# Score maxima two by two in TensorE's order, and none between the halves of the product with V

## Chip, cores and metric

The kernel runs on one core of one Trainium2 chip, as one launch. The metric is device time in microseconds (us). A core has five engines with instruction streams of their own, which meet only at semaphores: TensorE (PE in the profile), VectorE (DVE), ScalarE (ACT), GpSimd (POOL) and SyncE (SP), which issues most DMAs.

## The reference, cut to what matters

The input is 8 rows of 512 tokens by 128 features. Each row goes through two attentions with 16 heads of 8 dimensions, both of them computed from the same normalized tokens, and one of them is followed by a mixture of one shared and eight routed experts.

```python
for each of the 8 rows x:                      # x: 512 x 128
    xn = layernorm(x)
    # attention 1: causal, weights 1 - tanh(energy)**2, divided by their sum, then @ Wo.T
    s  = attention_1(xn)
    # attention 2: full softmax over 512 keys, then + residual
    h  = rmsnorm(xn, norm1_w)
    X  = xn + softmax(q @ k.T * scale) @ v @ wo
    # feed-forward: shared expert + 8 experts, top 2 weighted by the router
    h2 = rmsnorm(X, norm2_w)
    g  = X + shared(h2) + sum_e combine[:, e] * (silu(h2 @ gate_e) * (h2 @ up_e)) @ down_e
    out = x + s * silu(g)
```

The softmax of attention 2 subtracts the maximum of each query's scores before the exponential. These maxima are what the change moves.

## The kernel before

**A row's stages on TensorE.** The kernel loops over the 8 rows. The first seven run in a hardware loop (`LOOP`, it = 0 to 6), the last one stands behind it (`LAST`), and a short prologue (`FIRST`) prepares row 0. Within a row TensorE's program has 28 attention units and then 9 experts.

Units 0 to 15 are attention 2 (stage 1): unit n computes, for 4 heads and one block of 128 keys, the transposed scores in two halves q of two heads each (`scores`, L951, two 64-row matmuls into S0 or S1, the heads r = 0 and r = 1 of a head pair at partitions 0 to 63 and 64 to 127), ScalarE takes the exponential (L522), and the product with V (`with_v`, L976) follows two units later. For most units that product is itself cut in two halves of 256 columns, each behind one half of the scores. Units 16 to 27 are attention 1 (stage 2), with the causal mask added by matmuls (L943) and VectorE forming the weights (L684); there the product with V is one piece, behind the first half of the scores.

An expert (`expert`) is 12 matmuls of 512 columns with all 128 rows, in four groups of three (L1013, L1014, L1015: the high and low parts of a split multiplication), and each group is one step. From expert 2 on, the second product of the expert two before it (L997) follows as steps 5 and 6, so that an expert has 6 steps, and 4 for experts 0 and 1.

**The maxima.** The maximum over 512 keys must be known before stage 1 of a row. `maximum` on TensorE (L918) multiplies Q and K of one head h and one tile t of 128 queries, 48 rows by 512 columns, into M0 or M1, and VectorE reduces the 512 columns to one (L647). A row has 64 of them (16 heads by 4 tiles), in the order of head pair, tile, head r: run X (head pairs 0 to 3, 32 maxima) is computed for the next row during the experts, and the runs Y and Z (head pairs 4 and 5, and 6 and 7, 16 maxima each) for this row in units 0 to 8. Neighbours in the order have different r: they read partitions 0 to 47 and 64 to 111. The finished maxima of a run are turned by one matmul (`maxT_X`, `maxT_Y`, `maxT_Z`, L924) and go by DMA into a row of Q's stack, so that the score matmul itself subtracts them.

**The two M buffers.** All small products of TensorE go through M0 and M1 in turn: the maxima, the projections, transposes of the outputs (`oT2`, `oT1`, L930), the router's logits (L1084), a suffix sum of V (`suffix`, L1090), the routing weights' transpose (`combT`, L1097). `begin` waits until the use two before has been read, and stops TensorE's whole stream there, since an engine works its program in order:

```python
k, _n = u(name)                  # M0 or M1, by turns
pe.wait_ge(*free(u, name))       # the use before the last has been read
```

**Placement.** The table `PLACES` gives the list of small works of each unit and expert; its order fixes the turns of M0 and M1 and the order in which VectorE and ScalarE read. Where inside a unit or expert a work stands in TensorE's order is decided in `row`, by cutting the list into as many pieces as there are steps, four in a unit. The lists of an X expert are: expert 2: x0 to x4; expert 3: oT1 2, oT1 3, x5 to x8; expert 4: x9, x10, V1, x11, ctxT1, x12; expert 5: x13, x14, proj1, x15 to x17; experts 6 and 7: six maxima each; expert 8: x30, x31, maxT_X. (x0 is the first maximum of run X.) VectorE reads the first 4 of a list of 6 ahead of its own product of an expert (L792), and the last 2 behind it.

Of the kernel before, what the change touches and what calls it, by code (L numbers as in the profile page):

```python
# [132 lines left out]
def program(nc, x, par, n1w, n2w, w1, w2, router, w_gu, w_dn, out):  # L133
# [4 lines left out]
    with ctx_:  # L138
# [745 lines left out]
        def _(pe):  # L884
# [48 lines left out]
            def scores(it, n, q):  # L933

                k, c = score_use(it, 2 * n + q)
                pe.wait_ge(s_read[k], c + 1)
                g, _kind, js = ATTENTION[n]
                key, query = ("K2", "Q2") if n < N1 else ("K1", "Q1")
                hp, at = 2 * g + q, 0
                if n >= N1:  # L940
                    for j in js:
                        for r in range(2):
                            t_.matmul(S[k][:, 512 * r + at:512 * r + at + 128], identb[:, :], never[:, :],  # L943
                                      start=(j == js[0]), stop=False, skip_group_check=True)
                        at += L - 128 * j
                    at = 0
                for j in js:
                    i0 = 0 if n < N1 else 128 * j
                    for r in range(2):
                        rows = slice(HALF * r, HALF * r + HALF)  # L950
                        last = t_.matmul(S[k][:, 512 * r + at:512 * r + at + L - i0],  # L951
                                         stack[key][rows, hp, 128 * j:128 * j + 128],
                                         stack[query][rows, hp, i0:L], start=n < N1, stop=True, skip_group_check=n >= N1)
                    at += L - i0
                last.then_inc(s_full[k], 1)

            def with_v(it, n, half=None):


                g, _kind, js = ATTENTION[n]  # L960
                G, V, w = (g, V2, width(n)) if n < N1 else (NG + g, V1, width(n))
                k, c = acc_use(it, G)
                if js[0] == 0:
                    pe.wait_ge(o_read[k], c + 1)
                if n >= N1:
                    pe.wait_ge(weighed, it * WEIGHED + 2 * (n - N1) + 2)
                elif half != 1:
                    for i in range(2):
                        pe.wait_ge(s_read[i], it * S_USES + n + 2)
                at = 0  # L970
                for j in js:
                    i0, i1 = (128 * j if n >= N1 else 0, L) if half is None else (half * L // 2, (half + 1) * L // 2)
                    if n < N1:
                        at = i0
                    for q in range(4):
                        last = t_.matmul(O[k][32 * q:32 * q + VW, i0:i1], V[:, j, 4 * g + q, :],  # L976
                                         PT[:, n % SLOTS, w * q + at:w * q + at + i1 - i0],
                                         start=(j == 0), stop=(NT - 1 in js and j == js[-1] and half != 0))
                    at += i1 - i0
                if half != 0:  # L980
                    last.then_inc(pv_done, 1)

            def routing_weights(it, e):
                k, c = acc_use(it, 2 * NG + 2 * e - 1)
                pe.wait_ge(o_read[k], c + 1)
                t_.matmul(O[k][:, :], sel[:, e - 1, :], cT[:, :], start=True, stop=True).then_inc(cb_full, 1)  # L986
# [119 lines left out]
            def first_scores(it):  # L1106

                pe.wait_ge(row_in["X"], (it + 1) * 64)
                for q in range(2):
                    scores(it, 0, q)  # L1110

            def row(u, it, following):
                order.clear()
                current[0] = u

                v_at = {n: n - 2 for n in range(2, N1 + 2)} | {n: n - 3 for n in range(N1 + 3, UNITS)}
                for n in range(UNITS):
                    if n == N1 - 1:
                        pe.wait_ge(setup, 2)
                    for run, (p0, _p1) in RUNS.items():  # L1120
                        if n == NT * (p0 // 2) and n:
                            pe.wait_ge(row_in[run], (it + 1) * 64)
                    if n == N1:
                        for name in ("Q1", "K1"):
                            pe.wait_ge(stacked[name], (it + 1) * 32 * len(PAIRS))
                    names = u.places[n]
                    for i in range(4):
                        if i % 2 == 0:
                            if n:
                                scores(it, n, i // 2)  # L1130
                        elif v_at.get(n, N1) < N1 and v_at[n] % NT > 0:
                            with_v(it, v_at[n], i // 2)
                        elif n in v_at and i == 1:
                            with_v(it, v_at[n])
                        for name in names[len(names) * i // 4:len(names) * (i + 1) // 4]:
                            work(u, it, name)
                with_v(it, UNITS - 3)
                pe.wait_ge(h2r_ready, it + 1)
                for e in range(NE):
                    names = u.places[EXPERT + e]  # L1140
                    steps = 6 if e >= 2 else 4
                    for i, _step in enumerate(expert(it, e)):
                        if e == 0 and i < 2:
                            with_v(it, UNITS - 2 + i)
                        for name in names[len(names) * i // steps:len(names) * (i + 1) // steps]:
                            work(u, it, name)
                routing_weights(it, NE - 1)
                for _step in second_product(it, NE - 2):
                    pass
                for t in range(NT):  # L1150
                    last = t_.matmul(O[0][:, t * 128:t * 128 + 128], x1[:, t, :], ident[:, :], start=False, stop=False)
                last.then_inc(down_done, 1)
                for _step in second_product(it, NE - 1):
                    pass
                if following:
                    first_scores(it + 1)
                work(u, it, "outT")
                assert order == u.order
# [8 lines left out]
            with pe.Fori(0, B - 1) as it:  # L1167
                row(LOOP.row(it), it, True)
            row(LAST, B - 1, False)


# [37 lines left out]
```

## Time and profile before

| | |
|---|---|
| median of 3 runs | 1283.97 us (1280.16 to 1283.98) |
| profiled execution, its own time | 1285.18 us |
| its span, first to last instruction | 1283.4 us |
| PE busy | 1141.4 us, 89% |
| DVE busy | 870.5 us, 68% |
| ACT busy | 687.7 us, 54% |
| POOL busy | 342.0 us, 27% |
| granted TensorE clock over the span | 0.939 of full speed |

A row of the batch takes 153.6 us on TensorE. "L918 MATMUL M<-stackK,stackQ" is the instruction at line 918 that writes M from the stacks of K and Q. A row of the timeline with "x4" holds four like instructions, and its duration is from the first one's start to the last one's end. "[0.79 <-DVE nmax L647]" says that the engine sat idle for 0.79 us until that instruction of VectorE released it. Matmul records begin when the matmul begins to stream, and last longer than the time after which the next one begins, because the array is a pipeline; the distance between starts is what counts.

### The profile page before, as it was taken

To read this page: it belongs to the slowest core of one execution; us is meant where nothing else is said; L and a number is where in the kernel's file an instruction comes from. 1 tells how busy PE (TensorE), PEld (TensorE's weight loads), DVE (VectorE), ACT (ScalarE), POOL (GpSimd) and SP (SyncE) were. 2 spreads that over 40 slices of the span, in tenths; PEclk is the share of its full clock that TensorE was granted. 3 is DMA by queue.
4 is the path that set the end of the run, shared out by engine and by line. 5 is a ranking of instruction groups with operands and counts; after the bars stand their busy time and mean duration, and the time that the engine had idled before them with its cause. 6 is when DMAs were issued, how large, how long until landed. Compare 5 with 4: busy or idle time off the path is not lost.

```text
span 1283.4 us, 21377 instructions
## 1 busy us (share of the span) xinstructions
PE 1141.4 (89%) x7176; PEld 493.3 (38%) x7176; DVE 870.5 (68%) x1702; ACT 687.7 (54%) x937; POOL 342.0 (27%) x180
## 2 busy tenths in 40 slices
PE   2379999899998899899998999989999899999998
PEld 1112454234541354324543245422454234542365
DVE  7366975669757686576865688656976568756682
ACT  4039822597226862378523883249722596227842
POOL 6400542014320333203421035210542014420013
PEclk9559999799997999989998999979999799998999
DMA  5510330004300042002310034000440004300000
GB/s 165 99 36 2 76 70 5 27 2 87 62 1 27 24 82 44 11 18 43 70 37 27 2 62 75 13 28 2 75 74 1 27 9 84 58 1 18 1 1 8
DMA packets 58626, 49.95 MB, mean 39 GB/s; under 512 B 6672, under 2 KB 58128, under 8 KB 58384
## 3 DMA queue, kind: packets, MB, share of 16 engines
q1 hardware_dynamic: 55744, 44.35, 18.1%
q10 hardware_dynamic: 2768, 4.06, 0.9%
q8 instruction: 74, 1.21, 0.4%
q14 instruction: 40, 0.33, 0.1%
HBM read 33.45 MB, written 14.68 MB: 37 GB/s over the span
## 4 chain that ended last, share of the span: by engine, by line
PE 61%; DVE 12%; issue 11%; ACT 9%; DMA 3%; SPq 2%; POOL 1%; DVEq 0%; ACTq 0%; POOLq 0%
PE M L918 11%; PE O L976 10%; PE O L997 10%; PE S L1013 7%; PE S L951 4%; PE S L1015 4%; PE S L1014 4%; ACT PT L522 4%; DVE PT L684 4%; DVE nmax L647 3%; PE M L1090 1%; DVE ht L670 1%; SPq L321 1%; PE M L911 1%; PE M L905 1%
## 5 line engine op out<-in xcount | busy, mean ns | idle before, releaser
L522 ACT ACTIVATE PT<-S 128x1024 f32<-128x1024 f32 (+1 forms) x448 | 421.2, 973 | 125.4 <-PE S L951 122.7
L647 DVE TENSOR_REDUCE nmax<-M 128x1 f32<-128x512 f32 x512 | 335.9, 687 | 197.0 <-PE M L918 193.2
L684 DVE SCALAR_TENSOR_TENSOR PT<-PT 128x768 f32<-128x768 f32 (+1 forms) x192 | 215.6, 1172 | 94.0 <-ACT PT L522 93.6
L918 PE MATMUL M<-stackK,stackQ 48*128 48x512 bf16 x512 | 218.3, 445 | 68.6 <-DMA stackK<-scrK 28.7
L976 PE MATMUL O<-PT,V 128*12 128x256 f32 (+3 forms) x2816 | 253.1, 441 | 0.0
L412 POOL TENSOR_TENSOR PT<-PT 128x1024 f32<-128x1024 f32 x56 | 133.0, 2376 | 376.3 <-ACT PT L531 376.3
L951 PE MATMUL S<-stackQ,stackK 64*128 64x512 bf16 (+3 forms) x1024 | 211.3, 368 | 15.7 <-DMA stackQ<-mTZ 7.4
L396 POOL TENSOR_TENSOR split<-split,parts 128x512 f32<-128x512 f32 x32 | 91.3, 2852 | 491.5 <-ACT parts L483 491.5
L531 ACT ACTIVATE PT<-O 128x512 f32<-128x512 f32 x64 | 38.2, 597 | 249.0 <-PE O L986 249.0
L918 PEld LDWEIGHTS M<-stackK,stackQ 48*128 48x128 bf16 x512 | 46.9, 95 | 308.7 <-issue 165.4
L997 PE MATMUL O<-PT,wdn 128*128 128x512 f32 x288 | 151.0, 623 | 0.0
L1013 PE MATMUL S<-h2hi,wgu_hi 128*128 128x512 f32 x288 | 139.9, 486 | 0.1
L1015 PE MATMUL S<-h2hi,wgu_lo 128*128 128x512 f32 x288 | 113.5, 394 | 0.0
L1014 PE MATMUL S<-h2lo,wgu_hi 128*128 128x512 f32 x288 | 113.2, 393 | 0.0
L565 ACT ACTIVATE PT<-S 128x1024 f32<-128x1024 f32 x72 | 74.0, 1027 | 55.3 <-PE S L1015 53.9
L792 DVE TENSOR_TENSOR PT<-PT,S 128x1024 f32<-128x1024 f32 x72 | 87.4, 1213 | 18.9 <-PE S L1015 17.2
L951 PEld LDWEIGHTS S<-stackQ,stackK 64*128 64x128 bf16 x1024 | 45.3, 94 | 92.8 <-ACT PT L522 56.7
L976 PEld LDWEIGHTS O<-PT,V 128*12 128x12 f32 x2816 | 47.1, 91 | 84.5 <-issue 80.8
L1013 PEld LDWEIGHTS S<-h2hi,wgu_hi 128*128 128x128 f32 x288 | 54.1, 188 | 54.3 <-issue 50.6
L943 PE MATMUL S<-never,identb 128*128 128x128 bf16 x512 | 61.2, 222 | 9.1 <-ACT PT L522 8.1
L943 PEld LDWEIGHTS S<-never,identb 128*128 128x128 bf16 x512 | 35.4, 99 | 70.3 <-ACT PT L522 43.1
L997 PEld LDWEIGHTS O<-PT,wdn 128*128 128x128 f32 x288 | 46.5, 189 | 34.5 <-issue 33.6
(183 smaller groups left out, 1067.0 us busy)
## 6 DMA issues: line engine op xcount, KB each, us to landing
stackQ<-scrQ SPq DMA_DIRECT2D x192, 64.0 KB
stackK<-scrK SPq DMA_DIRECT2D x192, 64.0 KB
scrQ<-parts SPq DMA_DIRECT2D x16, 384.0 KB, 2.5
scrK<-parts SPq DMA_DIRECT2D x16, 384.0 KB, 5.3
PT<-in_w_gu ACTq DMA_DIRECT2D x2, 1152.0 KB, 7.9
xin<-in_x SPq DMA_DIRECT2D x8, 256.0 KB, 2.9
xres<-in_x SPq DMA_DIRECT2D x8, 256.0 KB, 3.3
out<-xres SPq DMA_DIRECT2D x8, 256.0 KB, 2.3
```

The source lines that it names most:

```text
L412: g.tensor_tensor(a, a, w, ALU.mult).then_inc(routed, 1)
L522: a.activation(PT[:, n % SLOTS, 2 * q * w:2 * q * w + 2 * w].rearrange("p (r n) -> p r n", r=2), S[k][:, :].rearrange("p (r n) -> p r n", ...
L647: v.tensor_reduce(nmax[:, h % 2, h // 2, t:t + 1], M[k][:, :], AX.X, ALU.max, negate=True).then_inc(m_read[k], 1)
L684: v.scalar_tensor_tensor(p, p, 1.0, p, ALU.subtract, ALU.mult).then_inc(weighed, 1)
L918: t_.matmul(M[k][:, :], stack["Q2"][a:a + ROW_ADD, hp, t * 128:t * 128 + 128], stack["K2"][a:a + ROW_ADD, hp, :], start=True, stop=True).t ...
L943: t_.matmul(S[k][:, 512 * r + at:512 * r + at + 128], identb[:, :], never[:, :], start=(j == js[0]), stop=False, skip_group_check=True)
L951: last = t_.matmul(S[k][:, 512 * r + at:512 * r + at + L - i0], stack[key][rows, hp, 128 * j:128 * j + 128], stack[query][rows, hp, i0:L], ...
L976: last = t_.matmul(O[k][32 * q:32 * q + VW, i0:i1], V[:, j, 4 * g + q, :], PT[:, n % SLOTS, w * q + at:w * q + at + i1 - i0], start=(j == ...
L997: last = t_.matmul(O[0][:, :], wdn[:, e, f, :], AB[e % DEPTH][:, f * 512:f * 512 + 512], start=(e == 0 and f == 0), stop=(e == NE - 1 and ...
L1013: t_.matmul(dst, wgu_hi[:, e, cols], h2hi[:, :], start=True, stop=False)
L1014: t_.matmul(dst, wgu_hi[:, e, cols], h2lo[:, :], start=False, stop=False)
L1015: last = t_.matmul(dst, wgu_lo[:, e, cols], h2hi[:, :], start=False, stop=True)
```

## The change

TensorE's order alone changes. VectorE's, ScalarE's and SyncE's orders are the same, and so are all instructions and the turns of M0 and M1. In a unit the first half of the list now stands behind the first half of the scores and the second half of the list behind the second, both ahead of the product with V that follows. In an expert, works are placed behind steps 1, 3 and 5 only, in even numbers where the list allows it.

```diff
@@ attention units
-                        for name in names[len(names) * i // 4:len(names) * (i + 1) // 4]:
-                            work(u, it, name)
+                        if i % 2 == 0:
+                            for name in names[0:len(names) // 2] if i == 0 else names[len(names) // 2:]:
+                                work(u, it, name)
@@ experts
-                        for name in names[len(names) * i // steps:len(names) * (i + 1) // steps]:
-                            work(u, it, name)
+                        if i % 2 == 0:
+                            for name in names[len(names) * i // steps // 2 * 2:
+                                              len(names) if i + 2 >= steps else len(names) * (i + 2) // steps // 2 * 2]:
+                                work(u, it, name)
```

The same rule moves other works of the lists: `logits` of unit 27 goes ahead of the product with V, `suffix` of expert 0 ahead of that expert's last three matmuls, and oT1 0, combT and oT1 1 of expert 1 stand together behind step 3 instead of behind steps 2, 3 and 4. Expert 2 gets no work behind step 1, x0 and x1 behind step 3 and x2, x3, x4 behind step 5. maxT_X stands between the two last halves of expert 8's second product, instead of behind them.

TensorE's order in a unit of stage 1 (unit 3, products with V in halves), before:

```order
L951 MATMUL S0<-stackQ2,stackK2 128x512 x2
L918 MATMUL M1<-stackK2,stackQ2 128x512
L976 MATMUL O0<-PT,V2 12x256 x4
L893 REGISTER_ALU
L918 MATMUL M0<-stackK2,stackQ2 128x512
L951 MATMUL S1<-stackQ2,stackK2 128x512 x2
L918 MATMUL M1<-stackK2,stackQ2 128x512
L976 MATMUL O0<-PT,V2 12x256 x4
L893 REGISTER_ALU
L918 MATMUL M0<-stackK2,stackQ2 128x512
```

and with the change:

```order
L951 MATMUL S0<-stackQ2,stackK2 128x512 x2
L918 MATMUL M1<-stackK2,stackQ2 128x512
L893 REGISTER_ALU
L918 MATMUL M0<-stackK2,stackQ2 128x512
L976 MATMUL O0<-PT,V2 12x256 x4
L951 MATMUL S1<-stackQ2,stackK2 128x512 x2
L918 MATMUL M1<-stackK2,stackQ2 128x512
L893 REGISTER_ALU
L918 MATMUL M0<-stackK2,stackQ2 128x512
L976 MATMUL O0<-PT,V2 12x256 x4
```

The maximum that stood behind each half product with V has moved ahead of it, next to the one that was there.

TensorE's order in expert 5, difference of the two programs, around steps 1 and 2:

```order
 L986 MATMUL O<-cT,sel 128x512
 L893 REGISTER_ALU
-L918 MATMUL M<-stackK,stackQ 128x512
-L1013 MATMUL S<-h2hi,wgu_hi 128x512
-L1014 MATMUL S<-h2lo,wgu_hi 128x512
-L1015 MATMUL S<-h2hi,wgu_lo 128x512
-L918 MATMUL M<-stackK,stackQ 128x512
+L918 MATMUL M<-stackK,stackQ 128x512 x2
+L1013 MATMUL S<-h2hi,wgu_hi 128x512
+L1014 MATMUL S<-h2lo,wgu_hi 128x512
+L1015 MATMUL S<-h2hi,wgu_lo 128x512
```

The maximum that stood behind step 2 has moved ahead of that step's three matmuls, next to the one behind step 1. In experts 6 and 7 the same happens at steps 3 and 5 too, so that six single maxima become three pairs.

TensorE's order at the end of stage 2 (unit 27), with the change:

```order
L1029 REGISTER_ALU
L1084 MATMUL M1<-rts,h2T 128x8 x4
L966 REGISTER_ALU
L976 MATMUL O0<-PT,V1 12x128 x4
L976 MATMUL O0<-PT,V1 12x256 x4
L943 MATMUL S1<-never,identb 128x128 x4
```

Before, the two L976 stood ahead of L1084 (the logits, which wait until ScalarE has written h2T and h2hi).

## Rows read from the trace of the kernel before

**Rows 1.** Stretches of one row: PE, PEld, DVE, ACT, POOL busy; clock, DMA share, GB/s.
```profile
236.74:248.67 11.93, 11.16 (x56) 1.75 (x56) 8.20 (x13) 6.18 (x7) 0.00 (x0) 0.50 0.16 47
...
262.50:313.76 51.26, 46.58 (x448) 18.95 (x444) 37.71 (x82) 44.88 (x68) 15.87 (x7) 1.00 0.26 47
...
357.90:373.56 15.66, 15.66 (x48) 6.58 (x47) 10.38 (x14) 3.25 (x4) 4.75 (x2) 1.00 0.00 1
```

**Rows 2.** Timeline of PE in expert 7, a maximum between two groups.
```profile
367.74 0.40 PE L1015 MATMUL S<-h2hi,wgu_lo 128*128 128x512 f32 x1
...
368.39 0.50 PE L1013 MATMUL S<-h2hi,wgu_hi 128*128 128x512 f32 x1
368.72 0.39 PE L1014 MATMUL S<-h2lo,wgu_hi 128*128 128x512 f32 x1
```

**Rows 3.** Timeline of PE in expert 8, groups without one, and the row's end.
```profile
376.27 0.39 PE L1015 MATMUL S<-h2hi,wgu_lo 128*128 128x512 f32 x1
376.50 0.40 PE L1013 MATMUL S<-h2hi,wgu_hi 128*128 128x512 f32 x1
376.73 0.39 PE L1014 MATMUL S<-h2lo,wgu_hi 128*128 128x512 f32 x1
...
379.97 0.24 PE L924 MATMUL M<-identb,mhX 128*64 128x128 bf16 x1 [0.39 <-DVE mhX L657]
...
384.90 0.61 PE L951 MATMUL S<-stackQ,stackK 64*128 64x512 bf16 x4
```

**Rows 4.** Timeline of PE in stage 1 at the low clock.
```profile
245.61 0.60 PE L918 MATMUL M<-stackK,stackQ 48*128 48x512 bf16 x1
245.62 1.02 PE L951 MATMUL S<-stackQ,stackK 64*128 64x512 bf16 x2
...
246.58 1.05 PE L976 MATMUL O<-PT,V 128*12 128x256 f32 x8
```

**Rows 5.** Timeline of PE and DVE in stage 1 at the full clock.
```profile
257.57 0.39 PE L918 MATMUL M<-stackK,stackQ 48*128 48x512 bf16 x1
...
257.90 0.39 PE L918 MATMUL M<-stackK,stackQ 48*128 48x512 bf16 x1
258.00 2.48 DVE L647 TENSOR_REDUCE nmax<-M 128x1 f32<-128x512 f32 x4 [0.16 <-PE M L918]
...
258.22 0.62 PE L976 MATMUL O<-PT,V 128*12 128x256 f32 x8
258.77 0.39 PE L918 MATMUL M<-stackK,stackQ 48*128 48x512 bf16 x1
...
260.21 0.39 PE L918 MATMUL M<-stackK,stackQ 48*128 48x512 bf16 x1
```

**Rows 6.** Timeline of PE at unit 27, around the logits.
```profile
308.98 0.84 PE L976 MATMUL O<-PT,V 128*12 128x128 f32 x16
310.23 1.06 PE L1084 MATMUL M<-rts,h2T 128*128 128x8 f32 x8 [0.41 <-ACT h2hi L497]
```

**Rows 7.** Timeline of DVE and PE in experts 0 to 2.
```profile
319.23 1.22 DVE L792 TENSOR_TENSOR PT<-PT,S 128x1024 f32<-128x1024 f32 x1 [0.19 <-DVE topf L701]
...
321.01 0.69 DVE L739 TENSOR_TENSOR h2T<-M,cneg 128x512 f32<-128x512 f32 x1 [0.55 <-PE M L1090]
...
322.79 0.19 DVE L714 TENSOR_TENSOR comb<-lp,lq 128x32 f32<-128x32 f32 x1
...
323.41 1.04 PE L1097 MATMUL M<-ident,comb 128*8 128x128 f32 x8
...
327.83 2.12 DVE L670 TENSOR_TENSOR ht<-h2T,rden 128x128 f32<-128x128 f32 x1
...
330.60 0.39 PE L918 MATMUL M<-stackK,stackQ 48*128 48x512 bf16 x1 [0.79 <-DVE nmax L647]
```

**Rows 8.** Timeline of DVE in expert 3: the two outputs oT1 2 and 3.
```profile
335.33 0.17 DVE L665 TENSOR_TENSOR dsum<-M,dcorr 128x16 f32<-128x16 f32 x1 [0.86 <-PE M L930]
...
338.02 0.16 DVE L665 TENSOR_TENSOR dsum<-M,dcorr 128x16 f32<-128x16 f32 x1
```

## The prediction

> **What bounds the kernel now.** I read the shares of busy time first (PE 89%, DVE 68%), then one row of the batch by stretches, then the timelines inside them. Every full row takes 153.6 us, and seven of the eight carry all the moved work. In experts 6 and 7 PE is busy 15.66 of 15.66 us and DVE 10.38 [rows 1]: PE alone sets the pace there. In units 9 to 27 ACT is busy 44.88 of 51.26 us [rows 1] and the attention goes at its pace. In stage 1 the clock was granted at half (1.2 of 2.4 GHz) for the first 11.93 us after the row's start [rows 1], and PE sets the pace. At the full clock it is DVE: four maxima are read in 2.48 us, then it waits 0.16, and the pattern of two half units repeats after 260.21 - 257.57 = 2.64 us [rows 5]. So one change meets four limits.
>
> **What a maximum costs among the experts.** From L1015 to the L1014 of the next group takes 368.72 - 367.74 = 0.98 us with one maximum between them [rows 2], and 376.73 - 376.27 = 0.46 without one [rows 3]. A single maximum costs PE 0.52 us, though at this clock its own slot is about 0.22: four score matmuls of like size, two for each half of the array, lasted 0.61 us from first start to last end [rows 3], which is one matmul's 0.39 and one more slot of 0.22. Had they run one by one it would be 0.39 + 3 x 0.22 = 1.05. The other 0.30 is paid on going from full matmuls to those on part of the rows and back. A pair pays that once, and its two heads read different partitions, so its second member should be nearly free. The Trainium skill says the same of the cause (TensorEngine Tiling (Array Packing), Key Properties: a change of tiling mode drains the engine), and gives no price; by it as by the row, it is the groups that count and not the maxima.
>
> Counted in the lists, the 32 singles of run X become 17 groups (experts 2 to 8: 2, 2, 3, 3, 3, 3, 1; in experts 4 and 5 three maxima stay alone, behind V1, ctxT1 and proj1). 15 groups x 0.52 = **-7.7 us a row**. The pairs don't starve DVE in experts 6 and 7: six reads and the product fill 5.2 of the new 7.83 - 3 x 0.52 = 6.3 us (10.38 / 2 [rows 1]), and the tightest wait, for the buffer of the sixth maximum, ends some 0.2 us before PE comes to the next pair.
>
> **What it costs elsewhere, a row.**
> (a) Stage 1, full clock. Before, two of the four matmuls that stand between two half products are maxima on either side of the scores. Now both follow the scores, and the second waits until DVE has read the pair before it, with V queued behind it. From a maximum to V is 258.22 - 257.90 = 0.32, from V to the next matmul 258.77 - 258.22 = 0.55 [rows 5], one slot for the scores 0.22: a new pair can't start before 1.09 after the last one's second member. A read starts 0.43 after its maximum (258.00 - 257.57) and the second ends 0.43 + 0.62 + 0.69 = 1.74 after the first began, and frees its buffer at about 1.79. With x the lag of the second behind the first, x' = 1.79 - (x + 1.09), so x settles at 0.35 and the half unit at 1.44, against 1.32 now. DVE, saturated before, gets small gaps. About 8 half units: **+0.9**. ACT is close to its limit from unit 9 on and takes the delay on. At the low clock the four matmuls take 246.58 - 245.61 = 0.97 us in either order, and DVE has time: 0.
> (b) Logits. They wait for ACT's h2hi until 310.23 in any order. The V product that started at 308.98 and lasted 0.84 used that wait [rows 6]; now it stands behind the logits, and what follows comes **+0.8** later.
> (c) Experts 0 and 1. The suffix goes ahead of the matmuls that DVE's product needs: the product starts about 1.7 later than 319.23, and comb ends 322.98 - 319.23 - 0.55 = 3.2 after that [rows 7], at some 324.2 instead of 322.98. PE reaches combT at 323.3 now that oT1 0 stands directly ahead, and waits for comb. At the entry of expert 2 I find **+0.7**.
> (d) Expert 2. x2, x3, x4 stand together, and x4 needs the buffer that x2 fills. DVE comes to x0 only after L670, which took 2.12 us [rows 7] (GpSimd worked at the same time) and now starts later by the delay of (c). x2 can start at 0.6 after PE gets there, x4 1.2 after x2: a wait of **+1.8**. The wait of 0.79 at x2 that is there now [rows 7] goes: **-0.8**.
> (e) Expert 3. oT1 2 and 3 are sent together, but DVE needs 338.02 - 335.33 = 2.69 us for the first [rows 8]; the second frees the buffer of x6 0.5 us into its work, 1.4 us after PE stands at x6. **+1.4**, less 0.3 for a like wait now.
> (f) Expert 8. maxT_X waits for DVE's mhX 0.39 us now, with all of the second product ahead of it [rows 3]. With half of that (0.86) moved behind it, it waits 1.2: **+0.8**.
>
> Sum of a row: -7.7 + 0.9 + 0.8 + 0.7 + 1.0 + 1.1 + 0.8 = -2.4. Seven rows: -16.8. The last row has no run X, and pays (a) and (c): +1.6. Together -15.2. The profiled execution took 1285.2 in all, so it would be 1270.0; the median of the runs stood 1.2 under that execution, so the median should be about **1269 us**, 1.2% less.
>
> The waits (c) to (e) are the weakest. If all the waits of (c), (d) and (e) are hidden, -3.9 more a row; if they are as large again, the gain is gone. The gate of the clock is a smaller unknown: rows get shorter, so the low stretch can begin up to some us earlier or later against the work. One us more of it costs 1 - 1.44/1.95 = 0.26 us (1.95, the half unit at the low clock: 0.97 for the four matmuls and about as much for V, 1.05 long [rows 4]), under 0.5 a row.
>
> **Rivals.**
> 1. My forecast, with errors of half a us a row in (a) to (f): 1261 to 1277. Chance 0.52.
> 2. The waits don't form, or in part: VectorE gets through experts 1 to 3 in time. 1240 (none of them) to 1261. For: DVE has slack there on average. Against: the turns of M0 and M1 tie x4 to x2 and x6 to oT1 3 whatever the average. Chance 0.20.
> 3. The other side: the two members of a pair don't overlap between full matmuls. Then each of the 14 seconds costs a slot of 0.22: +3.1 a row, +21.6 in all, about 1290, slower than before. The gain is gone at the point where a merged group saves 0.36 instead of 0.52 (15.2 us over 7 x 14 pairs is 0.16 each). Against it stand the four scores in 0.61 us [rows 3], though they have no full matmul behind them at once. Chance 0.08.
> 4. The waits are larger: x4, x6 and combT hold PE while everything behind them is ready, and stage 1 starves ACT. Twice (c) to (e) is +3.9 a row, 1296; half of that excess gives 1283. Chance 0.15, for 1277 to 1296.
> 5. The matmuls run strictly in order, and a maximum on the same half of the array as the next score costs a slot of its own. The change would then save a slot per half unit in stage 1 too: at the low clock 0.43 x 6 = 2.6 a row, so 1251. The Trainium skill has such a rule (TensorE: Matmul & The Clock Gate, What overlaps and what doesn't: matmuls start and end in program order). The trace speaks against it for this place: in units 0 to 4 the order is head 0's maximum, head 0's and head 1's scores, head 1's maximum, in order three slots of 0.43 or 1.28, and the block took 0.97 with the way to V in it [rows 4], two slots. Chance 0.05.
>
> **How the numbers follow.** No change is what lies within 0.3%, 1280 to 1288, about what runs of this kernel can tell. Faster: 1 and 2 and 5 wholly and a fifth of 4, 0.80. Same: 0.09, from 4. Slower: 0.11, from 3 and the rest of 4. The range of 8 in 10 goes from 1250 to 1282, over most of rival 2 and the near half of rival 4; the likeliest case alone has 1261 to 1277.
>
> **What the profile after would show.** Experts 6 and 7 at 6.3 us each instead of 7.83, the pair's two L918 some ns apart, and 0.98 from L1015 to L1014 with a pair between: if it is 1.2, rival 3 holds. L918 waiting on DVE nmax at the third maximum of expert 2, and on DVE h2T L666 in expert 3, of about 1.8 and 1.4 us: without them rival 2. L1097 waiting on comb, L924 on mhX 1.2 us. Half units at full clock of 1.44 us; at the low clock 1.95 as now, and if 1.5, rival 5. The forecast is wrong above all if DVE's place in experts 1 to 3 isn't what I took it for.

## The result, and the profile after

The change makes the kernel slower, by 0.7%, clear of the noise. Its median is 1293.19 us (1286.59 to 1299.57, 11 runs) against 1283.98 (1280.16 to 1286.33, 11 runs) of the kernel before in the same session: a ratio of 1.0073, 95% interval 1.0052 to 1.0095. The forecast was 1269 us, a gain of 1.2%. The profiled execution took 1299.57 us, the longest of the 11, with a span of 1297.8; its rows overstate the median's loss by some 5 us.

The page of the changed kernel: busy time by engine, the granted clock in 40 slices, and the group of the maxima.

```profile
PE 1134.9 (87%) x7176; PEld 504.2 (39%) x7176; DVE 866.9 (67%) x1702; ACT 687.2 (53%) x937; POOL 339.5 (26%) x180
...
PEclk9559999798997999999997998979999798997999
...
L918 PE MATMUL M<-stackK,stackQ 48*128 48x512 bf16 x512 | 172.4, 451 | 77.6 <-DMA stackK<-scrK 26.1
```

TensorE is busy 6.5 us less than before and the span is 14.4 us longer: the pairs save work, and idle time and a lower clock (0.920 over the span, 0.939 before) take more than that back.

Where this happens is seen when a row is cut at landmarks in TensorE's order. The numbers are differences of starts in the timeline (the row's first maximum, in the first row its first score matmul; the first L943, where stage 2 begins; L1084, the logits; the first L1013 of experts 0 and 8; the row's last transpose), in us, as means over the seven rows of the loop. The columns on the right are experiments told below.

| stretch | before | after | logits_alone | logits_filled | logits_back | stage1_alone | experts_only | tuned |
|---|---|---|---|---|---|---|---|---|
| row start to stage 2 | 39.5 | 41.5 | 39.1 | 38.4 | 40.5 | 40.0 | 38.8 | 38.3 |
| stage 2 to logits | 34.4 | 35.0 | 34.4 | 34.4 | 35.0 | 34.4 | 34.4 | 34.4 |
| logits to expert 0 | 3.5 | 6.8 | 6.3 | 4.4 | 3.5 | 3.5 | 3.5 | 3.5 |
| expert 0 to expert 8 | 59.8 | 55.2 | 59.8 | 59.8 | 55.2 | 59.8 | 55.2 | 54.4 |
| expert 8 to the end | 13.2 | 13.7 | 13.2 | 13.2 | 13.7 | 13.2 | 13.7 | 12.9 |

After less before: +1.9, +0.6, +3.3, -4.6 and +0.5, a sum of +1.7 a row. With the 0.1 between rows that is +1.75, 12.3 us over seven rows; the last row is 4.3 longer, and the first begins 2.2 earlier: the 14.4 of the spans.

**The experts went as forecast.** The changed kernel in expert 7, timeline of PE, and the window of an expert (PE, PEld, DVE, ACT, POOL busy; clock, DMA share, GB/s):

```profile
373.47 0.40 PE L1015 MATMUL S<-h2hi,wgu_lo 128*128 128x512 f32 x1
373.80 0.39 PE L918 MATMUL M<-stackK,stackQ 48*128 48x512 bf16 x2
374.12 0.50 PE L1013 MATMUL S<-h2hi,wgu_hi 128*128 128x512 f32 x1
374.45 0.39 PE L1014 MATMUL S<-h2lo,wgu_hi 128*128 128x512 f32 x1
```

```profile
367.80:374.10 6.30, 6.30 (x25) 3.25 (x23) 4.91 (x7) 1.64 (x3) 2.40 (x2) 1.00 0.00 0
```

"x2 | 0.39" is two matmuls from the first one's start to the second one's end, no longer than one alone. From L1015 to the next L1014 it takes 374.45 - 373.47 = 0.98 us, as with a single maximum in [rows 2]: the second is free. The expert takes 6.30 instead of 7.83.

**The logits did not.** The changed kernel at the end of stage 2, timeline of PE, and the windows up to the logits and behind them:

```profile
314.10 1.76 PE L1084 MATMUL M<-rts,h2T 128*128 128x8 f32 x8 [1.19 <-ACT h2hi L497]
315.79 1.48 PE L976 MATMUL O<-PT,V 128*12 128x128 f32 x16
...
321.58 0.50 PE L1013 MATMUL S<-h2hi,wgu_hi 128*128 128x512 f32 x1
```

```profile
310.00:314.10 4.10, 2.11 (x20) 0.97 (x17) 4.00 (x10) 4.10 (x8) 2.43 (x1) 1.00 0.57 88
314.10:321.50 7.40, 7.40 (x42) 3.24 (x42) 5.44 (x8) 3.17 (x7) 7.04 (x3) 0.54 0.27 40
```

The wait has grown from 0.41 [rows 6] to 1.19 us, which is the V product's way, as forecast. What wasn't forecast is the clock behind it: 0.54 of full speed in the second window, 1.00 in the first. The logits take 1.76 us instead of 1.06 and the V product 1.48 instead of 0.84. Before, the clock stood at 1.00 here, and in the 4.10 us up to the logits TensorE was busy for 2.89 us instead of 2.11. In each of the seven rows of the changed kernel a stretch at half clock (1.2 of 2.4 GHz) begins 0.05 to 1.8 us behind the logits' start; it lasts 3.4 us in three rows and 6.8 in four.

**Waits that were forecast among the experts**, timeline of PE, all four places of one row:

```profile
332.06 1.04 PE L1097 MATMUL M<-ident,comb 128*8 128x128 f32 x8 [0.47 <-DVE comb L714]
...
339.21 0.39 PE L918 MATMUL M<-stackK,stackQ 48*128 48x512 bf16 x1 [0.33 <-DVE nmax L647]
339.80 0.39 PE L918 MATMUL M<-stackK,stackQ 48*128 48x512 bf16 x1 [0.21 <-DVE nmax L647]
340.40 0.39 PE L918 MATMUL M<-stackK,stackQ 48*128 48x512 bf16 x1 [0.21 <-DVE nmax L647]
...
346.49 0.39 PE L918 MATMUL M<-stackK,stackQ 48*128 48x512 bf16 x1 [1.14 <-DVE h2T L666]
...
382.84 0.24 PE L924 MATMUL M<-identb,mhX 128*64 128x128 bf16 x1 [1.15 <-DVE mhX L657]
```

combT waits 0.47 us, the maxima of expert 2 0.75 in three pieces, x6 behind the two outputs 1.14, and maxT_X 1.15. These are idle times; a wait that ends while the record of the matmul before it still runs is counted in part or not at all. By their starts x4 comes 340.40 - 339.21 = 1.19 us behind x2.

**Stage 1 pays too.** Timeline of PE at the full clock:

```profile
262.07 0.39 PE L951 MATMUL S<-stackQ,stackK 64*128 64x512 bf16 x2
262.30 0.38 PE L918 MATMUL M<-stackK,stackQ 48*128 48x512 bf16 x1
262.86 0.39 PE L918 MATMUL M<-stackK,stackQ 48*128 48x512 bf16 x1 [0.19 <-DVE nmax L647]
...
263.74 0.39 PE L951 MATMUL S<-stackQ,stackK 64*128 64x512 bf16 x2
263.96 0.48 PE L918 MATMUL M<-stackK,stackQ 48*128 48x512 bf16 x2
...
264.93 0.39 PE L951 MATMUL S<-stackQ,stackK 64*128 64x512 bf16 x2
```

Two half units take 264.93 - 262.07 = 2.86 us, 1.43 each, where two took 2.64 [rows 5]. Not each of them waits: one has its second maximum 0.56 behind the first and V behind that, the next has both together.

More is lost at the half clock, at the start of a row. Its first maximum and its first two products with V, before:

```profile
236.37 0.60 PE L918 MATMUL M<-stackK,stackQ 48*128 48x512 bf16 x1 [2.96 <-issue]
...
240.28 1.90 PE L976 MATMUL O<-PT,V 128*12 128x512 f32 x8
...
244.63 1.05 PE L976 MATMUL O<-PT,V 128*12 128x256 f32 x8
```

and with the change:

```profile
237.23 0.60 PE L918 MATMUL M<-stackK,stackQ 48*128 48x512 bf16 x1 [3.41 <-issue]
...
241.94 1.90 PE L976 MATMUL O<-PT,V 128*12 128x512 f32 x8
...
246.73 1.05 PE L976 MATMUL O<-PT,V 128*12 128x256 f32 x8
```

The first product comes 4.71 us behind the row's first maximum instead of 3.91, the second 9.50 instead of 8.26. From there to the end of the half-clock stretch the distance stays: the half units take some 1.95 us in both kernels.

### The profile page after: what moved, and what is told of

Read it like the earlier page. It is cut to its first block, busy times and chain, and to the rows that moved or that the text cites. A ratio compares the mean times of both kernels' runs of the same rounds, so it can differ in the third digit from the quotient of the medians.

```text
span 1297.8 us, 21377 instructions
## 1 busy us (share of the span) xinstructions
PE 1134.9 (87%) x7176; PEld 504.2 (39%) x7176; DVE 866.9 (67%) x1702; ACT 687.2 (53%) x937; POOL 339.5 (26%) x180
## 4 chain that ended last, share of the span: by engine, by line
PE 57%; DVE 15%; issue 13%; ACT 9%; DMA 2%; SPq 2%; POOL 1%; DVEq 0%; ACTq 0%; POOLq 0%
PE O L976 11%; PE O L997 9%; PE M L918 8%; DVE nmax L647 5%; PE S L1013 5%; PE S L951 5%; PE S L1015 4%; PE S L1014 4%; DVE PT L684 4%; ACT PT L522 3%; PE M L905 2%; PE M L1090 1%; SPq L321 1%; PE M L911 1%; DVE ht L670 1%
## 5 line engine op out<-in xcount | busy, mean ns | idle before, releaser
L647 DVE TENSOR_REDUCE nmax<-M 128x1 f32<-128x512 f32 x512 | 330.0, 686 | 173.5 <-PE M L918 169.5
L684 DVE SCALAR_TENSOR_TENSOR PT<-PT 128x768 f32<-128x768 f32 (+1 forms) x192 | 220.2, 1192 | 106.5 <-ACT PT L522 105.9
L976 PE MATMUL O<-PT,V 128*12 128x256 f32 (+3 forms) x2816 | 260.3, 452 | 0.0
L918 PE MATMUL M<-stackK,stackQ 48*128 48x512 bf16 x512 | 172.4, 451 | 77.6 <-DMA stackK<-scrK 26.1
L396 POOL TENSOR_TENSOR split<-split,parts 128x512 f32<-128x512 f32 x32 | 85.1, 2659 | 507.4 <-ACT parts L483 507.4
L951 PE MATMUL S<-stackQ,stackK 64*128 64x512 bf16 (+3 forms) x1024 | 188.2, 373 | 15.7 <-DMA stackQ<-mTZ 7.2
L531 ACT ACTIVATE PT<-O 128x512 f32<-128x512 f32 x64 | 38.3, 599 | 231.2 <-PE O L986 231.2
L1013 PE MATMUL S<-h2hi,wgu_hi 128*128 128x512 f32 x288 | 146.8, 510 | 0.2
L918 PEld LDWEIGHTS M<-stackK,stackQ 48*128 48x128 bf16 x512 | 40.1, 96 | 216.4 <-DVE nmax L647 103.6
L1015 PE MATMUL S<-h2hi,wgu_lo 128*128 128x512 f32 x288 | 113.5, 394 | 0.0
L1014 PE MATMUL S<-h2lo,wgu_hi 128*128 128x512 f32 x288 | 112.9, 392 | 0.0
L976 PEld LDWEIGHTS O<-PT,V 128*12 128x12 f32 x2816 | 47.7, 92 | 89.1 <-issue 80.5
L1013 PEld LDWEIGHTS S<-h2hi,wgu_hi 128*128 128x128 f32 x288 | 54.0, 188 | 56.0 <-issue 45.1
L943 PE MATMUL S<-never,identb 128*128 128x128 bf16 x512 | 63.0, 227 | 9.4 <-ACT PT L522 7.5
L943 PEld LDWEIGHTS S<-never,identb 128*128 128x128 bf16 x512 | 33.2, 99 | 91.8 <-ACT PT L522 46.3
L1014 PEld LDWEIGHTS S<-h2lo,wgu_hi 128*128 128x128 f32 x288 | 54.4, 189 | 15.8 <-issue 11.5
```

The lines of the kernel that those rows point to most:

```text
L647: v.tensor_reduce(nmax[:, h % 2, h // 2, t:t + 1], M[k][:, :], AX.X, ALU.max, negate=True).then_inc(m_read[k], 1)
L684: v.scalar_tensor_tensor(p, p, 1.0, p, ALU.subtract, ALU.mult).then_inc(weighed, 1)
L918: t_.matmul(M[k][:, :], stack["Q2"][a:a + ROW_ADD, hp, t * 128:t * 128 + 128], stack["K2"][a:a + ROW_ADD, hp, :], start=True, stop=True).t ...
L1013: t_.matmul(dst, wgu_hi[:, e, cols], h2hi[:, :], start=True, stop=False)
L1014: t_.matmul(dst, wgu_hi[:, e, cols], h2lo[:, :], start=False, stop=False)
L1015: last = t_.matmul(dst, wgu_lo[:, e, cols], h2hi[:, :], start=False, stop=True)
```

## Experiments

Three sessions, each with its own runs of the kernel before (1282.35, 1282.19 and 1282.55 us).

**Halves of the change.** `experts_only` has the new placement in the experts and the old one in the units; `units_only` the reverse.

```diff
@@ units_only
+                        if i % 2 == 0:
+                            for name in names[0:len(names) // 2] if i == 0 else names[len(names) // 2:]:
+                                work(u, it, name)
@@ experts_only
+                        if i % 2 == 0:
+                            for name in names[len(names) * i // steps // 2 * 2:
+                                              len(names) if i + 2 >= steps else len(names) * (i + 2) // steps // 2 * 2]:
+                                work(u, it, name)
```

> The experts' works placed as in the change, the units' as before. Theory A (the experts gain what was worked out, 4.1 us a row, and the units lose it again, most of it through a new stretch at half clock behind the logits): the stretch before expert 0 is as before, no half clock there, and the time is about 1284 - 7 x 4.1 + 0.7 = 1256 us. Theory B (shorter rows only shift the low stretches of the clock, so that any gain in the experts is given back): 1275 to 1290.

> The units' works placed as in the change, the experts' as before. Theory A: the units alone cost what the change lost and the experts' gain too, about 9 + 28 = 37 us, so about 1320 us, with a half-clock stretch behind the logits in every row but the last. Theory B: no more than the worked out 1.7 us a row, about 1297.

Measured: `experts_only` 1254.96 us (1251.92 to 1255.30), 0.9773 [0.9755, 0.9792]; `units_only` 1312.58 (1309.49 to 1315.88), 1.0231 [1.0209, 1.0254]. A gain of 27.4 us and a loss of 30.2. All of the gain of the change is in the experts, and the units lose more than it. The two don't add up to the change: together they make +2.8, and the change cost 9.4 (0.0073 x 1282.35). In the profiled executions logits to expert 0 takes 6.8 us and the way to stage 2 41.5 in the changed kernel, against 6.1 and 40.2 in `units_only`; the half-clock stretches of the changed kernel are longer.

**The logits alone, and the change without them.** `logits_alone` is the kernel before with the new cutting in unit 27 only; `logits_back` is the changed kernel with the old cutting in unit 27.

```diff
+                        if n == UNITS - 1:
+                            if i % 2 == 0:
+                                for name in names[0:len(names) // 2] if i == 0 else names[len(names) // 2:]:
+                                    work(u, it, name)
+                            continue
```

> The kernel before with one edit: in unit 27 the logits stand ahead of the product with V. Theory A: TensorE idles over 1 us at the logits, the clock is granted at half soon after, and a row gets 2.5 to 4 us longer: 1301 to 1312. Theory B: only the uncovered product counts, 0.8 a row: about 1290, clock as before.

> The change with one edit undone: in unit 27 the logits stand behind the product with V again. Theory A: the half-clock stretch before expert 0 is gone and the time is 1293 less some 3.2 x 7 = 22, about 1271, that is the forecast. Theory B: 0.8 a row less, about 1288.

Measured: `logits_alone` 1305.50 us (1302.57 to 1311.43), 1.0189 [1.0166, 1.0212]. `logits_back` 1269.65 (1265.32 to 1272.06), 0.989 [0.987, 0.991]. The logits on the other side of a product of 0.84 us cost 23.2 us (1305.50 - 1282.35); taken out of the change they give some 22 back (1.0073 x 1282.35 - 1269.65). In the rows of the trace logits to expert 0 is 2.8 us longer, 20 in all; the profiled execution was 2.9 us below its median. `logits_alone`, timeline and window:

```profile
313.81 1.06 PE L1084 MATMUL M<-rts,h2T 128*128 128x8 f32 x8 [1.18 <-ACT h2hi L497]
314.80 0.84 PE L976 MATMUL O<-PT,V 128*12 128x128 f32 x16
...
316.18 1.96 PE L905 MATMUL M<-xnT,w1s 128*128 128x512 f32 x2
```

```profile
313.80:319.90 6.10, 6.08 (x43) 2.23 (x43) 5.10 (x9) 3.67 (x8) 5.92 (x2) 0.72 0.12 21
```

Here the half clock comes in a little later (the logits and V at their full speed, then 1.96 instead of 1.13 for L905), and it comes in every row of the loop. In `logits_back` there is none behind the logits, and L1084 to expert 0 takes 314.27 - 310.74 = 3.53 us as before:

```profile
310.74 1.06 PE L1084 MATMUL M<-rts,h2T 128*128 128x8 f32 x8 [0.41 <-ACT h2hi L497]
...
314.27 0.50 PE L1013 MATMUL S<-h2hi,wgu_hi 128*128 128x512 f32 x1
```

**The wait filled.** So far the longer idle time and the half clock came and went together. `logits_filled` is `logits_alone` with five more matmuls of 512 columns ahead of the logits, into the same buffer, which the logits then overwrite. They change no order; they only keep TensorE at work while ScalarE finishes.

```diff
+                    k = begin(u, name)
+                    for j in range(5):
+                        t_.matmul(M[k][:, :], identb[:, :], stack["K1"][:, j % HP, :], start=True, stop=True)
                     wait_read(u, "h2T", name)
-                    k = begin(u, name)
```

> The kernel with only the logits moved ahead of the product with V, and in the wait that this opens TensorE runs five matmuls of 128 rows by 512 columns into the logits' buffer, which the logits then overwrite (nothing of the result changes). Theory A (the idle time brings the half clock, and the half clock costs more than the wait): no half clock behind the logits, 4.4 us from logits to expert 0 instead of 5.9 to 7.4, and 1282 + 7 x 0.85 = 1288 us against 1305.5. Theory B (the half clock comes from what follows, or the wait itself costs the 3.3 us a row): about 1305, or more by the added matmuls.

Measured: 1284.15 us (1280.69 to 1285.67), 1.0007 [0.9993, 1.002], 21.4 less than `logits_alone`, by adding work. Timeline and window:

```profile
304.96 1.25 PE L1083 MATMUL M<-stackK,identb 128*128 128x512 bf16 x5
306.21 1.06 PE L1086 MATMUL M<-rts,h2T 128*128 128x8 f32 x8
```

```profile
306.21:310.60 4.39, 4.39 (x43) 2.07 (x42) 4.39 (x7) 2.57 (x5) 4.39 (x1) 1.00 0.58 85
```

The clock is 1.00 and logits to expert 0 takes 4.39 us in every row. This parts the two costs: 4.39 - 3.53 = 0.86 is the V product that lost its cover, the forecast's 0.8; the other 6.35 - 4.39 = 1.96 a row in `logits_alone` (2.4 in the changed kernel) is the half clock. That the total is no longer than before's, though 0.86 x 7 = 6 us were added, goes with row starts that are 1.2 us shorter on average, with half-clock stretches of 6.8 and 10.2 us in place of 13.65, in a profiled execution that was itself 3.3 us below its median; why they are shorter isn't known.

**Stage 1 alone.** The kernel before with the new cutting in units 0 to 15 (the condition is `n < N1`).

> The kernel before, with only the works of units 0 to 15 placed as in the change. Theory A (the prediction's term: the second maximum of a pair waits for VectorE, 0.9 a row, only at full clock): 1282 + 8 x 0.9 = 1289 us. Theory B (the pairs cost at the low clock as well, 1.5 a row at an equally long low stretch, as the stretches of the changed kernel suggest): 1294 or more.

Measured: 1292.03 us (1290.02 to 1295.35), 1.0083 [1.0067, 1.0099], so 9.8 us slower. What PE waited for in stage 1 of one row, for this kernel and for `tuned`, whose stage 1 is that of before, both rows with a half-clock stretch of 6.8 us at their start (us in total, times, longest):

```profile
PE M L918 <- DVE nmax L647: 2.7, 10, 0.5
```

```profile
PE M L918 <- DVE nmax L647: 1.4, 4, 0.6
```

Waits for VectorE's reads grow by 1.3 us and from 4 to 10 in number, and the way to stage 2 by 39.5 - 37.9 = 1.6. Most of the loss is this wait. The time lies between the two theories; the 1.6 us at an equal stretch is what theory B had.

**Shorter reads.** If the loss is the wait for the read, it should go when the read is short. `short_reads_before` is the kernel before, with VectorE reading 256 of the 512 columns of the maxima of Y and Z (half of each of those maxima is left out); `short_reads_stage1` is `stage1_alone` with the same.

```diff
-                v.tensor_reduce(nmax[:, h % 2, h // 2, t:t + 1], M[k][:, :], AX.X, ALU.max, negate=True).then_inc(m_read[k], 1)
+                v.tensor_reduce(nmax[:, h % 2, h // 2, t:t + 1], M[k][:, 0:(512 if name in MAX["X"] else 256)], AX.X, ALU.max, negate=True).then_inc(m_read[k], 1)
```

> The kernel before, with VectorE reading only 256 of the 512 columns for the maxima of runs Y and Z (the other half is left out of the maximum). It is the base for short_reads_stage1. A read takes about 0.42 instead of 0.69 us, VectorE no longer bounds stage 1 at the full clock: 1282 less up to 1 us a row, 1275 to 1282.

> The kernel stage1_alone with the same short reads. Theory A (what the pairs cost in stage 1 is the wait of the second member for VectorE's read): the difference to short_reads_before falls from 10 us to under 3. Theory B (it comes from where the first and last maxima stand, where PE starts the row with two in a row, or from the T matmuls): still 8 or more.

Measured: 1247.92 us (1247.44 to 1248.51), 0.9731 [0.9714, 0.9747], and 1259.27 (1257.80 to 1265.89), 0.9831 [0.9796, 0.9867]. The pairs still cost 11.3 us. In one row of each, the waits for reads in stage 1:

```profile
PE M L918 <- DVE nmax L647: 0.3, 1, 0.3
```

```profile
PE M L918 <- DVE nmax L647: 0.6, 2, 0.3
```

The listed idle time grows by only 0.3 us, and the way to stage 2 by 0.9 (36.0 against 35.1 on average). The other 0.6 stands at the start of the row. `short_reads_before`, the last maximum ahead of the first product with V:

```profile
232.52 0.61 PE L918 MATMUL M<-stackK,stackQ 48*128 48x512 bf16 x1
233.06 1.90 PE L976 MATMUL O<-PT,V 128*12 128x512 f32 x8
```

`short_reads_stage1` at the same place:

```profile
235.72 1.17 PE L918 MATMUL M<-stackK,stackQ 48*128 48x512 bf16 x2
236.82 1.90 PE L976 MATMUL O<-PT,V 128*12 128x512 f32 x8
```

The first product starts 236.82 - 232.92 = 3.90 us behind the row's first maximum, against 233.06 - 229.72 = 3.34: one maximum more stands ahead of it. The two of that pair don't start together. The first starts at 235.72; VectorE's read of the buffer that the second needs, 0.42 us from 235.80 on, ends at 236.22, and the second starts at 236.29. The record of the first still runs until 236.32, so the list has no idle time here. The short reads didn't take the wait away at this place, which is why the loss stayed at 11 us where theory A had under 3.

The first kernel also shows what the forecast never asked: VectorE's reads in stage 1 are worth 34.6 us, where up to 7 were expected. Of the 4.4 us a row (39.5 to 35.1) 2.9 are left when rows with an equal half-clock stretch are compared (37.9 to 35.0); the rest goes with shorter stretches.

**Taking only the pairs that pay.** `tuned` has the units and experts 0 and 1 of before, pairs behind steps 1, 3 and 5 of experts 2 to 7, and in expert 8 maxT_X behind all of the second product. `tuned_e2` also moves x4 of expert 2 behind the last step.

```diff
-                        for name in names[len(names) * i // steps:len(names) * (i + 1) // steps]:
+                        if e < 2:
+                            cuts = [len(names) * j // steps for j in range(steps + 1)]
+                        else:
+                            c = [len(names) * j // steps // 2 * 2 for j in (0, 2, 4)] + [len(names)]
+                            cuts = [0, c[1], c[1], c[2], c[2], c[3], c[3]]
+                        if e == NE - 1:
+                            cuts[5] = len(names) - 1 if following else len(names)
+                        for name in names[cuts[i]:cuts[i + 1]]:
```

> Units, experts 0 and 1 as before, experts 2 to 7 as in the change, expert 8's pair as in the change and maxT_X behind the whole second product. Theory A: experts_only less the wait of combT and the late product (0.8 a row) and the wait of maxT_X (0.5 to 0.8): about 1255 - 10 = 1245 us. Theory B (those waits only move to expert 2 and 3, where VectorE is late anyway): 1250 to 1255.

> The kernel tuned, with x4 of expert 2 behind the last step instead of with x2 and x3. Theory A: x4 no longer waits 0.2 + 0.2 us for VectorE but costs a change of its own of 0.52: the same as tuned within 0.1%. Theory B (the third member holds the stream up by over 1 us): 5 us less than tuned.

Measured: `tuned` 1234.91 us (1232.59 to 1236.78), 0.963 [0.9613, 0.9646], the fastest of all; `tuned_e2` 1235.89 (1233.51 to 1238.42), 0.9639 [0.9623, 0.9656], the same. `tuned` is 47.3 us under before: 5.7 a row from the experts (table: 5.4 + 0.3), 40 in all, and most of the rest from row starts 1.2 us shorter, which nothing in the edit explains except where the half-clock stretch ends. Theory A stood at 1245; over `experts_only` the experts give 1.6 a row and 0.7 in the last one, 12 instead of 10 us, and the rest is again the length of the half-clock stretches. x4's wait costs no more than the change between matmuls that taking it out costs.

**Both of a pair on the same half of the array.** `same_half` is `tuned` with every maximum computed from partitions 0 to 47 (those of the odd heads are then another head's).

```diff
-                a, hp = HALF * (h % 2), h // 2
+                a, hp = 0, h // 2
```

> The kernel tuned, with the maxima of head 1 of each pair computed from head 0's partitions too (so half of the maxima are another head's), and so both members of a pair use the same half of the array. Theory A (the two members ran at the same time before, and a slot is 0.22 us): each of 14 pairs a row costs a slot more, 1235 + 7 x 14 x 0.22 = 1257 us, and experts 6 and 7 take 6.29 + 3 x 0.22 = 6.95 us each. In stage 1 a block of two maxima and two scores may take three slots too, at the low clock 0.43 more a half unit, so up to 1265. Theory B (they follow each other anyway and only the toll counts): 1235.

Measured: 1290.98 us (1281.02 to 1295.95, nine runs; a tenth took 1301.05), 1.0058 [1.0027, 1.0089], 56 us more than `tuned` and far above the 1257 to 1265 expected. Timeline of PE in an expert, in stage 1 at the half clock, and a window at a row's start:

```profile
365.26 0.39 PE L1015 MATMUL S<-h2hi,wgu_lo 128*128 128x512 f32 x1
...
365.82 0.60 PE L918 MATMUL M<-stackK,stackQ 48*128 48x512 bf16 x2
```

```profile
246.65 1.05 PE L976 MATMUL O<-PT,V 128*12 128x256 f32 x8
...
249.01 1.05 PE L976 MATMUL O<-PT,V 128*12 128x256 f32 x8
```

```profile
236.80:262.00 25.20, 24.19 (x108) 4.10 (x108) 14.39 (x23) 11.41 (x12) 0.00 (x0) 0.50 0.09 27
```

The pair takes 0.60 us instead of 0.39: one slot of 0.21 more, as the forecast's rival 3 had it, and an expert 6.9 instead of 6.3. The experts are 2.0 us a row longer, 14 in all, of the 56. In stage 1 a half unit at the half clock takes 249.01 - 246.65 = 2.36 us instead of 1.95, a slot of 0.41 more where maxima and scores share a half. Most of the rest is the clock again: in five of the eight rows the half clock lasts until 22 to 27 us behind the row's start, and these rows take 44 to 46.5 us to stage 2; the two with a stretch of 6.8 take 38.3, against 37.9 in `tuned`. Why the stretch is longer isn't shown.

## Why the prediction was wrong

**Removed singles, right.** -7.7 a row by 15 groups of 0.52 (15 x 0.52 is 7.8). The price of a group held to the digit (0.98 from L1015 to L1014, with a pair between), and experts 6 and 7 take 6.3. Experts 4 and 5, with one and two singles removed and no new wait, are 0.52 and 1.02 us shorter. The Trainium skill says that tiles of the array work at the same time (TensorEngine Tiling (Array Packing), Key Properties), and the pair in 0.39 us agrees, with 0.60 for two on the same half as the counter-example.

**(c) to (f), right in their sum, partly by luck.** The experts to the row's end were forecast at -4.1 (-7.7 + 0.7 + 1.0 + 1.1 + 0.8), and measured 55.2 - 59.8 + 13.7 - 13.2 = -4.1. combT's wait of 0.47, x6's of 1.14 (1.4 forecast) and maxT_X's of 1.15 (1.2) are at their places. With 0.52 added back for each single removed, experts 0 and 1 are 0.9 us longer ((c), 0.7 forecast), expert 2 0.5 ((d), 1.0), expert 3 1.2 ((e), 1.1) and expert 8 to the row's end 1.0 ((f), 0.8). That is 3.6 in all, the forecast's sum, with errors that cancel. In (d) x4 does stand 1.2 behind x2, but x2 waits 0.3 and not 0.6, and x4 would need 0.2 of its own in any case. `experts_only` is these terms alone: -4.1 x 7 + 0.7 for the last row is -28.0 from 1282.35, so 1254.3, and it took 1254.96. That it comes so near is luck in part: in its profiled execution the row starts are 0.7 us a row shorter as well, and the last row is 3.2 longer instead of 0.7.

**(b) Logits, the step that failed.** The forecast priced the uncovered V product at 0.8, and `logits_filled` measures that at 0.86. It then set the clock aside as "a smaller unknown", and thought only of the stretch at the row's start. Yet the row was there: TensorE stood idle for 0.41 us there [rows 6], was busy for 2.89 of the 4.10 us up to the logits, and the edit took the only work out of that wait. With 1.19 us of idle time the granted clock fell to half behind it in every row. Measured for the whole step: 23.2 us alone, 3.3 a row, four times the term. Less its term (0.8 x 7 = 5.6) that is 17.6 of the 24.2 us between forecast and result. The rest is (a), 9.8 instead of 7.2, and what was left out, 0.6 x 7 = 4.2, below. That these sum to 24.4 is better than they can promise, as the parts don't quite add (see the halves of the change).

The Trainium skill describes a clock that changes between its levels when short idle times stand between groups of matmuls (TensorE: Matmul & The Clock Gate, A second HAM failure mode: psum-queue depth-cycling). This trace agrees: with 1.99 us idle out of 4.10 the clock fell, and with the wait filled it didn't.

**(a) Stage 1, too small and mostly at the wrong place.** The half unit of 1.43 us at the full clock stands in the trace (1.44 forecast), and the waits for reads with it. But `stage1_alone` costs 9.8 us, and the term was 0.9 x 8 = 7.2. The forecast put the half clock at nothing, because the four matmuls of a half unit take 0.97 us in either order. That holds only once the half products with V alternate with them: by the second product of a row the changed kernel is 9.50 - 8.26 = 1.2 us behind, at the half clock. Two rows in which the half clock ends 12.3 us behind the first maximum, one of each kernel, take 40.8 and 39.4 us to stage 2, so that 1.4 is the whole loss there, and 1.2 of it is this. ([rows 1] begins at 236.74; the row's first maximum is at 236.37.)

**Left out.** Units 16 to 27 are cut by the same rule, and the way from stage 2 to the logits grew by 0.6 us a row. No term of the sum had them. In the trace of `logits_back` the products with V of unit 16 come 0.6 us later, now behind the transposes of xn, and from 19 us into the stage on everything stands 0.56 later than before; which of the works in between costs it wasn't isolated.

**The rivals.** Rival 3 (a pair's members don't overlap) is refuted by the 0.39 and by `same_half`. Rival 5 (strict order in stage 1, half units of 1.5 at the low clock) is refuted by `stage1_alone`, which is slower and not faster, and `same_half` shows what its slot costs where it is paid: 2.36 us a half unit instead of 1.95. Nor is the order strict in the records: in [rows 4] a maximum and a score matmul start 0.01 us apart, and by its semaphore update that score matmul is the second of the two, on the other half of the array; the first starts 0.4 later, together with the next maximum. Rival 2 (no waits) is refuted by the four waits shown. Rival 4 had the number in its range (1277 to 1296) but not the cause: the waits among the experts came to the forecast's 3.6 and not to more, and of its other half, stage 1, only 2.6 us were above the forecast. Rival 3's 1290 is near too, and wrong in its cause. The case that happened, a covered wait laid bare and the clock lost behind it, was no rival at all. It should have been the one on the other side.

## What to carry to other kernels

Matmuls on part of the rows, strewn singly between full ones, cost 0.52 us each here at the full clock, and two of them on different halves cost the same 0.52: group them, in even numbers and on different halves. Before moving a work away from a wait, price not only the work but the idle time that it leaves, and look in the trace afterwards at the granted clock behind it: here 0.8 us more of idle time, in a stretch in which TensorE was busy for half of the time, cost two us more behind it. And a rule that pays at one place should be tried apart at each place: this one, applied everywhere, made the kernel 0.7% slower, and where it pays 3.7% faster.

## What the runs showed of the hardware that was unexpected

- 1.18 or 1.19 us of idle time in front of the logits, with TensorE busy 2.11 of the 4.10 us up to them, came with half clock in all rows of the loop in three kernels (the changed one, `units_only`, `logits_alone`), beginning between 0.4 us ahead of the logits' start and 2.6 behind it; 0.41 us of it, or five filling matmuls of 1.25 us (busy 3.30 of the 4.10), by none in the rows of the loop.
- Useless work made a kernel 1.6% faster (`logits_alone` to `logits_filled`, 1305.50 to 1284.15).
- In every kernel TensorE stands idle for 2.9 to 3.6 us at the turn of the hardware loop, and the clock falls between 2.6 us ahead of the new row's first maximum and 0.9 behind it. Ahead of the last row, which stands behind the loop, there is no such idle time, and the clock falls 1.0 to 4.1 us behind its first maximum. It can stay down under steady work: 24.19 us busy of the 25.20 in the window of `same_half`, all at half clock.
- The half-clock stretch at a row's start varies with what comes before and in it: 13.65 us in nearly all rows of before, 6.8 in most of `tuned`, up to 17.1 in the changed kernel and 27 in `same_half`. The way to stage 2 goes with it (with the units of before: 37.9 us at 6.8, 39.3 at 13.65). A few us of a kernel's time are decided there, and no run here isolates by what.
- The same VectorE instruction, L670 on 128x128, took 1.99 us with GpSimd's multiplication beside it and 0.29 in its next run 2.6 us later (346.63 - 344.03). The difference is more than the whole of x6's wait of 1.14. The rows, DVE and POOL in expert 3 of the changed kernel:

```profile
344.03 1.99 DVE L670 TENSOR_TENSOR ht<-h2T,rden 128x128 f32<-128x128 f32 x1
...
346.63 0.29 DVE L670 TENSOR_TENSOR ht<-h2T,rden 128x128 f32<-128x128 f32 x1
```

```profile
343.49 2.38 POOL L412 TENSOR_TENSOR PT<-PT 128x1024 f32<-128x1024 f32 x1 [1.38 <-ACT PT L531]
```
